# The last expert's second weights by column quarters, and the last group given back between first chunks

## The reference

```python
def _L3_ffn_ref(x, gate_w, gate_b, w1, w2):
    logits = jnp.einsum('bsd,ed->bse', x, gate_w) + gate_b
    probs = jax.nn.softmax(logits, axis=-2)
    vals_t, idx_t = jax.lax.top_k(probs.transpose(0, 2, 1), K)          # K = 8
    vals = vals_t.transpose(0, 2, 1)
    ...
    merged = jnp.einsum('bked,bke->bed', tok, vals)                     # one row per batch row and expert
    h = jnp.einsum('bei,eih->beh', jnp.concatenate([merged, ones], -1), w1)   # 512 -> 2048
    h = jax.nn.gelu(h, approximate=False)
    o = jnp.einsum('bej,ejo->beo', jnp.concatenate([h, ones], -1), w2)        # 2048 -> 512
    out_tok = jnp.einsum('beo,bke->bkeo', o, vals).reshape(b, K * E, d)
    out = jnp.zeros_like(x).at[jnp.arange(b)[:, None], flat_idx].add(out_tok)
    return out
x = x + _L3_ffn_ref(_layernorm(x, axis=-1), L3_ffn_gate_w, L3_ffn_gate_b, L3_ffn_w1, L3_ffn_w2)
```

## Time and profile before

| | us |
|---|---|
| median of three runs | 3422.64 |
| the profiled execution, its own time | 3418.8 |
| its span | 3417.1 |
| ring chunk, median from issue to landing (256 chunks) | 27.1 |
| last expert: first product | 3.64 |
| last expert: second product | 3.76 |
| last expert: given back | 3.70 |
| group 7 given back | 6.29 |
| one add of a tile, 128 x 512 | 0.69 |
| a store of 256 KB, issue to landing | 2.0 |

### The profile page before, as it was taken

How to read it: one execution, slowest core, us unless ns; L and a number is a source line. 1 busy time by engine, 2 the same in 40 slices (tenths; PEclk the granted TensorE clock), 3 DMA queues, 4 the chain that set the end, 5 groups by cost and what they waited for, 6 DMA issues and landing times. The chain is left out here.

```text
span 3417.1 us, 44590 instructions
## 1 busy us (share of the span) xinstructions
PE 3111.4 (91%) x18185; PEld 1699.2 (50%) x18185; DVE 1225.8 (36%) x2574; ACT 710.0 (21%) x1365; POOL 448.9 (13%) x436
## 2 busy tenths in 40 slices
PE   9999999998999999999999999999999997666676
PEld 6776643334444544444567675346886742111111
DVE  3766520003454579765241223114555220000000
ACT  2443101111333331110112130104441311000000
POOL 4452011221000000001000000005441000000000
PEclk9999999999999999999999999999999999878878
DMA  3102156844110212220641203970103069999999
GB/s 108 47 34 78 45 222 224 301 149 167 52 71 25 77 43 68 87 99 25 237 158 47 85 27 146 421 298 33 37 13 149 16 270 417 420 420 420 420 420 375
DMA packets 106074, 576.69 MB, mean 169 GB/s; under 512 B 25304, under 2 KB 34521, under 8 KB 47769
## 3 DMA queue, kind: packets, MB, share of 16 engines
q1 hardware_dynamic: 93104, 498.99, 36.9%
q0 software_dynamic: 12272, 75.26, 6.1%
q10 hardware_dynamic: 536, 0.14, 0.0%
HBM read 641.89 MB, written 9.50 MB: 191 GB/s over the span
## 5 line engine op out<-in xcount | busy, mean ns | idle before, releaser
L3094 PE MATMUL banks<-ring,h 128*32 128x512 f32 x1024 | 168.6, 767 | 81.2 <-DMA ring<-in_L_ffn_w 56.0
L3077 PE MATMUL banks<-ring,mine 128*32 128x512 f32 x1024 | 168.0, 699 | 50.3 <-DMA ring<-in_L_ffn_w 50.0
L924 PE MATMUL banks<-ring 128*128 128x256 f32 x784 | 179.9, 381 | 0.0
L434 POOL TENSOR_TENSOR rstd_pairs<-var_eps_pairs,minus_half 128x4 f32<-128x4 f32 x30 | 30.9, 1029 | 1068.0 <-DVE var_eps_pairs L422 904.2
L509 PE MATMUL banks<-normed_features,first 128*128 128x256 f32 x768 | 167.2, 379 | 0.4 <-ACT normed_features L476 0.4
L1839 PE MATMUL banks<-ring,xT 128*64 128x512 f32 x736 | 162.4, 599 | 5.5 <-DMA ring<-in_L_ffn_Wg,weight_row_of_slot 5.5
L3205 DVE COPY mine<-mT 128x32 f32<-128x32 f32 x31 | 5.6, 181 | 445.0 <-PE banks L3077 445.0
L924 PEld LDWEIGHTS banks<-ring 128*128 128x128 f32 x784 | 144.6, 190 | 28.6 <-issue 11.4
L509 PEld LDWEIGHTS banks<-normed_features,first 128*128 128x128 f32 x768 | 145.4, 190 | 21.6 <-issue 2.0
L3094 PEld LDWEIGHTS banks<-ring,h 128*32 128x32 f32 x1024 | 26.7, 122 | 193.2 <-DMA ring<-in_L_ffn_w 140.8
L897 PE MATMUL banks<-big 128*128 128x512 f32 x256 | 116.5, 599 | 0.0
(11 more groups left out here) (675 smaller groups left out, 5341.0 us busy)
## 6 DMA issues: line engine op xcount, KB each, us to landing
ring<-in_L_ffn_w SPq DMA_DIRECT2D x256, 1024.0 KB, 27.1
wb<-in_L_ffn_W SPq DMA_DIRECT2D x32, 1024.0 KB, 18.3
first<-in_L_ffn_W SPq DMA_DIRECT2D x16, 1024.0 KB, 14.7
second<-in_L_ffn_W SPq DMA_DIRECT2D x12, 1024.0 KB, 18.6
ctxT<-in_ctxT SPq DMA_DIRECT2D x8, 1024.0 KB, 5.0
big<-in_ctx SPq DMA_DIRECT2D x8, 1024.0 KB, 6.8
big<-in_ctxT SPq DMA_DIRECT2D x8, 1024.0 KB, 4.9
ring<-in_L_attn_Q_W SPq DMA_DIRECT2D x16, 512.0 KB, 3.5
```

What stands on the lines that cost most here:

```text
L434: pool.tensor_tensor(m.rstd2[:, 2 * half:2 * half + 2, :].rearrange("p t i -> p (t i)"), m.den2[:, 2 * half:2 * half + 2, :].rearrange("p ...
L924: ins = pe.matmul(halves(n % 2)[:, r, :], a, x, start=(k == 0), stop=(k == 1))
L3077: ins = pe.matmul(ps[B4 * q:B4 * q + B4, 0, :], mine[:, e % 2, k, :], w[:, q * 512:(q + 1) * 512], start=(k == 0), stop=(k == C - 1))
L3094: ins = pe.matmul(ps[B4 * q:B4 * q + B4, 2, :], h[:, Q * n + q, :], w[:, q * D:(q + 1) * D], start=(n == 0), stop=(n == Q - 1))
```

## The change

`Ring.by_columns` picks out the last four chunks, those of the second weights of expert 31. Each is now a quarter of the output columns (128 of 512) with all 2048 input rows. The array in device memory keeps its layout, so a quarter is read in runs of 512 bytes, as four DMAs of 256 KB; `there` expects four increments of 16.

On PE, the fold of expert 30 stands between the first and the second chunk of expert 31, and the giving back of group 7 between the second and the third (`fold`, `give`). The second product of expert 31 makes 16 matmuls of 128 columns for each quarter, into a bank of its own (`free`: banks 2, 0, 1, 3). Quarter n - 1 is given back after the matmuls of quarter n (`give_last`), each with its own copy by ACT. The first three quarters accumulate in banks 4 to 7; the last goes to the first 128 columns of the banks 2, 0, 1 and 3.

DVE first adds the four tiles in all 512 columns, once the third quarter has been given back, and then the four tiles' last 128 columns again from the four free banks. SP stores columns 0 to 383 of all tiles in one DMA after the first four adds, and columns 384 to 511 in another after the last.

```diff
@@ -2663,17 +2663,24 @@
         self.before = [s.made for s in self.landed]
         self.d = m.d
 
+    def by_columns(self, i):
+
+        return i // 4 == 2 * self.d["L3_ffn_w2"].shape[0] - 1
+
     def load(self, i):
 
         e, k = divmod(i, 8)
         if k < 4:
             return self.landed[i % RING], (self.slots[:, i % RING, :], self.d["L3_ffn_w1"][e, k])
+        if self.by_columns(i):
+            part = self.slots[:, i % RING, :].rearrange("p (n q c) -> p n q c", n=4, q=4)
+            return self.landed[i % RING], *[(part[:, n], self.d["L3_ffn_w2"][e, n][:, :, (k - 4) * P:(k - 3) * P]) for n in range(4)]
         return self.landed[i % RING], (self.slots[:, i % RING, :].rearrange("p (q n) -> p q n", n=D),
                                        self.d["L3_ffn_w2"][e, k - 4])
 
     def there(self, i):
 
-        return self.landed[i % RING].sem, self.before[i % RING] + 16 * (i // RING + 1)
+        return self.landed[i % RING].sem, self.before[i % RING] + 16 * (i // RING + (4 if self.by_columns(i) else 1))
 
 
 def L3_attn(m, chunks, gate_loads, bo):
@@ -3029,6 +3036,7 @@
         ps = m.ps
         hq, part, o4, spread = (m.y[:, i, :] for i in range(4))
         both = m.yT[:, 0:2, :]
+        free = (2, 0, 1, 3)
         up_done = lambda e: consumed.at(8 * e + 4)
         down_done = lambda e: consumed.at(8 * e + 8)
 
@@ -3037,10 +3045,10 @@
             for i in range(RING, 8 * E):
                 sp.wait_ge(*consumed.at(i - RING + 1))
                 start_loads(sp, chunks.load(i))
-            for t in range(T):
-                sp.wait_ge(*added.at(t + 1))
-                sp.dma_start(m.out[:, t, :], m.x[:, t, :]).then_inc(*stored.up(16))
-            sp.wait_ge(*stored.at(16 * T))
+            for i, cols in enumerate((slice(0, D - P), slice(D - P, D))):
+                sp.wait_ge(*added.at(T * (i + 1)))
+                sp.dma_start(m.out[:, :, cols], m.x[:, :, cols]).then_inc(*stored.up(16))
+            sp.wait_ge(*stored.at(32))
 
         @block.tensor
         def _(pe):
@@ -3068,9 +3076,33 @@
                 for c in range(C):
                     ins = pe.transpose(ps[:, 2 + half, c * P:(c + 1) * P], both[:, half, c * P:(c + 1) * P], m.ident[:])
                 ins.then_inc(*m_turned.up())
+
+            def fold(e):
+                pe.wait_ge(*parts_copied.at(e + 1))
+                pe.matmul(ps[B4 * (e % G4):B4 * (e % G4) + B4, 3, :], fold32[:], part, start=True, stop=True).then_inc(*folded.up())
+
+            def give(g):
+                pe.wait_ge(*spread_ready.at(g + 1))
+                pe.wait_ge(*o_ready.at(g + 1))
+                for t in range(T):
+                    pe.matmul(ps[:, 4 + t, :], spread[:, t * P:(t + 1) * P], o4, start=False, stop=False)\
+                      .then_inc(*given.up())
+
+            def give_last(n):
+                cols = slice(n * P, (n + 1) * P)
+                pe.wait_ge(*parts_copied.at(E + n))
+                for t in range(T):
+                    out = ps[:, 4 + t, cols] if n < Q - 1 else ps[:, free[t], 0:P]
+                    pe.matmul(out, spread[:, t * P:(t + 1) * P], part[:, cols], start=(n == Q - 1), stop=(n >= Q - 2))\
+                      .then_inc(*given.up())
+
             for e in range(E):
                 pe.wait_ge(*mine_ready.at(e + 1))
                 for k in range(C):
+                    if e == E - 1 and k == 1:
+                        fold(e - 1)
+                    if e == E - 1 and k == 2:
+                        give(groups - 1)
                     pe.wait_ge(*chunks.there(8 * e + k))
                     w = chunks.slots[:, (8 * e + k) % RING, :]
                     for q in range(Q):
@@ -3087,6 +3119,21 @@
                     ins = pe.transpose(ps[:, 1, n * P:(n + 1) * P], hq[:, n * P:(n + 1) * P], m.ident[:])
                 ins.then_inc(*h_turned.up())
                 pe.wait_ge(*h_ready.at(e + 1))
+                if e == E - 1:
+                    for n in range(Q):
+                        pe.wait_ge(*chunks.there(8 * e + 4 + n))
+                        w = chunks.slots[:, (8 * e + 4 + n) % RING, :]
+                        for i in range(4):
+                            for q in range(Q):
+                                ins = pe.matmul(ps[B4 * q:B4 * q + B4, free[n], 0:P], h[:, Q * i + q, :],
+                                                w[:, (Q * i + q) * P:(Q * i + q + 1) * P], start=(i == 0), stop=(i == 3))
+                        ins.then_inc(*consumed.up())
+                        if n == 0:
+                            pe.wait_ge(*spread_ready.at(groups + 1))
+                        else:
+                            give_last(n - 1)
+                    give_last(Q - 1)
+                    continue
                 for n in range(Q):
                     pe.wait_ge(*chunks.there(8 * e + 4 + n))
                     w = chunks.slots[:, (8 * e + 4 + n) % RING, :]
@@ -3096,21 +3143,10 @@
                     ins.then_inc(*consumed.up())
                 if e == 0:
                     pe.wait_ge(*fold_ready.at(1))
-                pe.wait_ge(*parts_copied.at(e + 1))
-                j, g = e % G4, e // G4
-                if e == E - 1:
-                    pe.wait_ge(*spread_ready.at(groups + 1))
-                    for t in range(T):
-                        pe.matmul(ps[:, 4 + t, :], spread[:, t * P:(t + 1) * P], part, start=False, stop=True)\
-                          .then_inc(*given.up())
-                    continue
-                pe.matmul(ps[B4 * j:B4 * j + B4, 3, :], fold32[:], part, start=True, stop=True).then_inc(*folded.up())
-                if j == G4 - 1 or e == E - 2:
-                    pe.wait_ge(*spread_ready.at(g + 1))
-                    pe.wait_ge(*o_ready.at(g + 1))
-                    for t in range(T):
-                        pe.matmul(ps[:, 4 + t, :], spread[:, t * P:(t + 1) * P], o4, start=False, stop=False)\
-                          .then_inc(*given.up())
+                if e < E - 2:
+                    fold(e)
+                    if e % G4 == G4 - 1:
+                        give(e // G4)
 
         @block.scalar
         def _(act):
@@ -3142,8 +3178,14 @@
                         act.dma_start(keb[B4 * j:B4 * j + B, groups], m.kept_rows[E - 1]).then_inc(*kept_read.up(16))
                 act.wait_ge(*biased.at(e + 1))
                 act.activation(h[:, :, 0:B], pre[:], ACT.Gelu).then_inc(*h_ready.up())
-                act.wait_ge(*down_done(e))
-                act.activation(part, ps[:, 2, :], ACT.Copy).then_inc(*parts_copied.up())
+                if e < E - 1:
+                    act.wait_ge(*down_done(e))
+                    act.activation(part, ps[:, 2, :], ACT.Copy).then_inc(*parts_copied.up())
+                else:
+                    for n in range(Q):
+                        cols = slice(n * P, (n + 1) * P)
+                        act.wait_ge(*consumed.at(8 * e + 4 + n + 1))
+                        act.activation(part[:, cols], ps[:, free[n], 0:P], ACT.Copy).then_inc(*parts_copied.up())
 
         @block.gpsimd
         def _(pool):
@@ -3212,8 +3254,12 @@
                         dve.wait_ge(*given.at(T * g))
                     dve.tensor_copy(o4, ps[:, 3, :]).then_inc(*o_ready.up())
             for t in range(T):
-                dve.wait_ge(*given.at(T * groups + t + 1))
+                dve.wait_ge(*given.at(T * (groups + Q - 2) + t + 1))
                 dve.tensor_tensor(m.x[:, t, :], m.x[:, t, :], ps[:, 4 + t, :], ALU.add).then_inc(*added.up())
+            dve.wait_ge(*added.at(T))
+            for t in range(T):
+                dve.wait_ge(*given.at(T * (groups + Q - 1) + t + 1))
+                dve.tensor_tensor(m.x[:, t, D - P:D], m.x[:, t, D - P:D], ps[:, free[t], 0:P], ALU.add).then_inc(*added.up())
 
 
 def L1_layer(m):
```

## The result

The kernel after takes 3428.94 us (median of 19 runs, 3419.81 to 3437.49), the one before 3422.64 (19 runs, 3416.51 to 3430.14). The ratio is 1.0018, 95% interval 1.0010 to 1.0026, so about 6.2 us slower, between 3.4 and 8.9. The profiled execution has a span of 3428.2.

A forecast was written before the change was run, and what follows sets the result against it. The prediction took the weight stream's last landing and the tail behind it as the bound. Order 0, loads +4.5, second product 0 and tail 0 us gave 3422.64 + 4.5 = 3427.1 us, range 3422.4 to 3430.3, counted as no change.

The forecast's parts named there:

- The bound: Last 600 us: a stream of weights PE waits for; the last chunk's landing and the tail behind it set the end.
- what the new order is worth: Fold and giving back between expert 31's first chunks: 0, with up to 1.4 us gained hidden by the wait for data.
- The loads, +4.5 us: Last 4 MB in runs of 512 bytes: 290 GB/s in place of 420, so the last landing comes 4.5 us later.
- SP's issues, 0: Sixteen load issues on SP in place of four, 0.63 us each at the median, hidden by the lead: 0.
- rival C: SP's issue paces the last quarters, deciding from 1.05 us a load; at 1.10 each, 7.6 us late, 3430.2; chance 0.13.
- The tail, 0: Behind the last landing L: PE's work passes to DVE's adds and the stores, L + 8.7 us, equal to before.
- A: Last loads: runs of 512 bytes cost nothing, landing as before, only the tail decides; 3422.6 us, chance 0.12.
- B: Last loads go at the burst rate, 344 GB/s, or engines' unequal ends even out: +2.2, 3424.8 us; chance 0.12.
- D: PE's clock at 1.2 GHz behind the last landing: last quarter and first give-back tile 1.3 us longer, 3428.4; chance 0.07.
- The signs: In the stream's end: 3.6 us a quarter, near 290 GB/s, PE waiting before the last two quarters, tail 8 to 9.7 us.

The follow-up runs named there:

- e1: Kernel before with only PE's order changed: fold of expert 30 and giving back of group 7 between expert 31's first chunks; ratio to before 1.0006.
- e4: Kernel after, with expert 31's second weights stored by column quarters in device memory, one DMA of 8 KB runs each; ratio to before 1.0004.
- e8: Kernel before, with each of the last four chunks loaded by two DMAs in runs of 1 KB; ratio to before 1.0011.
- e2: Kernel before, with each of the last four chunks loaded by four DMAs in runs of 512 bytes; ratio to before 1.0029.
- e3: Kernel before, with each of the last four chunks loaded by four DMAs in runs of 2 KB; ratio to before 1.0004.
- e11: Kernel after, unchanged, profiled once more and not timed; 24.5 us from expert 30's last chunk to the last quarter, tail 8.9 us.
- e9: e5 with three stores, columns 0 to 255 stored on their own ahead; median 3422.33 us beside 3424.99 of before, ratio 0.9992.
- e5: e4 with DVE's full adds before the quarters, then each quarter its own product, added in 128 columns as it comes; ratio to before 0.9999.
- e6: e5 with PE giving each quarter back before it waits for the next one; ratio to before 1.0002.
- e10: e2 with six idle PE matmuls behind each of the first three chunks of the last second product; ratio to before 1.0007.

## Why the prediction was right

- **The bound.** The stream of weights sets the last landing: in e1 PE is 3.5 us ahead of the trace before, and the last chunk is there no earlier. What I had wrong is what the new order is worth under that cover. I wrote that it makes expert 31's h ready earlier, by up to 1.4 us; at full clock the second product starts 13.7 us after expert 30's last chunk with it (e1, e4) and 13.3 without it (e8). The 3.5 us are the difference between half and full clock.
- **The loads, +4.5 us.** Measured 4.2 and 4.6 in two executions of after, and 4.2 in e2 with nothing else changed. The value came from sixteen loads of the same shape in a stage 2200 us earlier; the row with the full queue was the right one, and the peak of the earlier trace rows gave 2.2. The 512 bytes of the Trainium skill ("DMA: Bandwidth & Descriptors", Specifications) are no line rate here: e2, e8 and e3 show the cost going on to 1 and 2 KB. By its mechanism the term is a cost for each run, which the prediction took over as a rate without naming it.
- **SP's issues, 0.** Nearly right in the sum, wrong in the picture. SP stands in its sixteen issues in the kernel after like this:

```profile
L177 SPq DMA_DIRECT2D ring<-in_L_ffn_w x16: 633/830/8990, 3381.1 to 3414.0; - x16
...
DMA to landing us min/median/max: 4.2/4.9/22.8
```

  The second and the third small load held it 8.7 and 9.0 us, while large chunks left the queue, and the last landed only 5.2 us after its issue in place of 27. This is rival C's mechanism, and it cost little, since the DMA engines had work nearly all the time. From 3397 to 3417 their share is 0.95 or more in every microsecond but one:

```profile
3404.00:3405.00 1.00, 1.00 (x7) 0.21 (x9) 0.00 (x0) 0.00 (x0) 0.03 (x1) 1.00 0.95 245
3405.00:3406.00 1.00, 1.00 (x12) 0.26 (x8) 0.00 (x0) 0.00 (x0) 1.00 (x1) 1.00 0.74 186
```

  The last two numbers are the DMA share and GB/s. e11 has four such microseconds, with shares of 0.67 to 0.79, and its landing is 0.4 us later. Taken as lost time that is 0.3 us in after and 1.0 in e11, an estimate. C's point of decision, 1.05 us a load on SP, was the wrong measure: the sixteen issues took 33.7 us, 2.1 each, and the landing was not held up accordingly. Since a small load holds SP 0.63 us at the least, most of the 8.7 and 9.0 must be waiting for room; no run shows the two apart.
- **The tail, 0.** Measured +0.3 and +0.2. By its steps: full adds end at L + 4.0 (foreseen 4.2), small ones at L + 4.9 (5.6; 0.22 each, not 0.35), but the last store lands 3.6 us after its issue (2.7 foreseen). The stores of after, 3420 to 3428.2 us, rate in 40 slices:

```profile
GB/s 0 80 0 0 0 0 0 0 0 0 0 0 0 0 0 0 0 0 0 0 157 360 375 375 397 360 390 285 330 382 357 312 287 285 290 173 3 0 0 0
...
out<-x_tokens SPq DMA_DIRECT2D x1, 768.0 KB, 3.7
out<-x_tokens SPq DMA_DIRECT2D x1, 256.0 KB, 3.6
```

  Unlike the four in the earlier trace rows, the two stores move in one block of 3.1 us for 1.05 MB, 340 GB/s. The faster adds and the slower stores cancel: that the sum of the tail came out is in part luck.
- **Rivals.** A (runs of 512 bytes are free) and B (344 GB/s) fall by e2. D, the clock, did not strike in the tail of either trace of after, but it did in e2 and e8. In the first trace of after it was at half ahead of the last quarter: the second quarter took 1.46 for 1.08, and the giving back behind it 2.08 for 1.16. I had given D 1.3 us; where it struck, in the tail of the kernel before, it cost 2.3 and 3.5.
- **The signs.** The quarters start 3.5 and 3.4 us apart at the end, the rate is near 290, and the tail is within its bounds. PE waits 1.06 us for the last quarter but not at all for the third, since the low clock had kept it busy; in e11 it waits 1.75 and 1.29. One sign was badly chosen: in the span the last quarter starts 10.8 us later than 3408.4, beyond the 6 I had set. 6.6 of them are there already at expert 30's last chunk, and only the stretch behind it, 4.2, bears on the change.
- **The size.** 4.5 us were forecast, the stretches show 4.5 and 4.8 (e11), the timed runs 6.2 (3.4 to 8.9). The 1.7 between forecast and timed runs are within the interval. They could be the low clock in some of the runs, or the stages ahead; the profiles are too few to tell, and it stays open.

## What to carry to other kernels

At the end of a stream that is bound by DMA, work on what stands behind the last landing, and leave the shape of the last loads alone, or change the layout in memory with it: cutting a chunk by columns to shorten an 8.7 us tail cost 4.2 us of transfer and won nothing. To shorten the tail, take out of it what doesn't need the last piece (here the full adds and the early stores, 2.4 us), then look at what queues behind what. And look at the granted clock of the work behind the last landing before an operation's time in one trace is put down to an edit.

## What the runs showed of the hardware

- The last 4.19 MB came at 420 GB/s with runs of 8 KB, in 10.0 us, and with runs of 512 bytes in some 4.2 us more, about 295 GB/s. 2 KB cost 0.8 us and 1 KB 1.8 (e3, e8). A cost of about 8.5 ns for each run on each DMA engine fits them, an estimate.
- SP's queue held eleven loads of 128 runs (27 us ahead), but only some 5 us of loads with 512 runs; at the change SP stood 8.7 and 9.0 us in the second and third of them.
- A store of 256 KB landed 2.0 us after its issue where four of that size were issued 0.9 us apart (before, runs of 2 KB). With runs of 512 bytes it took 2.6 with 262 KB issued 0.9 us ahead (e9), 3.6 with 786 KB issued 0.9 ahead (after, e5), and 2.3 with 786 KB issued 2.5 ahead (e6).
- The granted clock fell to half, 1.2 GHz, in the last waits of e2 (1.10 and 2.32 us for a chunk) and e8 (1.52 us) and stayed there for 13 to 14 us. It added 2.3 and 3.5 us to a tail of 8.7. It stayed at 2.4 GHz where idle matmuls filled the waits (e10), but also in e1 with waits of 1.43 and 1.42 us, and it fell in the trace before with none over 1.44.
